# The last stage's normalisations, done in the last units of the layers for 13 of 16 batches

## The reference

```
h  = layernorm(x)                                   # 16 batches
for 4 layers:                                       # 16 heads of 64
    q = norm(h) Wq / 8 ; k = ctx Wk ; v = ctx Wv
    bias = relu(dist * Wth + bth) . Wto + bto + mask    # 32 terms per layer
    h = h + softmax(q k' + bias) v Wo
    h = h + relu(norm(h) Wf1 + bf1) Wf2 + bf2
x1 = x + tanh(g_xattn) * norm(h)                    # gated sum
f  = layernorm(x1)
out = x1 + tanh(g_ffn) * (attention(f, 16 heads of 8) + top-2 of 8 experts(f))
```

## Time and profile before

| | us |
|---|---|
| median of 3 runs (lowest, highest) | 1273.55 (1273.51, 1273.87) |
| profiled execution | 1273.89 |
| its span | 1272.1 |
| busy: PE | 1155.1 (91%) |
| busy: DVE | 1103.9 (87%) |
| busy: ACT | 1070.1 (84%) |
| busy: POOL | 804.0 (63%) |

### The profile page before, as it was taken

The page is one execution under the profiler, slowest core; times in us unless marked ns, Lnnn a source line. Parts: engine busy times, 40 slices in busy tenths (PEclk is TensorE's granted clock), DMA queues, the critical chain, the costliest instruction groups (busy, mean ns, idle before and its releaser), DMA issues.

```text
span 1272.1 us, 35758 instructions
## 1 busy us (share of the span) xinstructions
PE 1155.1 (91%) x11216; PEld 989.3 (78%) x11216; DVE 1103.9 (87%) x4455; ACT 1070.1 (84%) x3387; POOL 804.0 (63%) x917
## 2 busy tenths in 40 slices
PE   1499999999999999999999999999999999899897
PEld 1478888888888888888888888888888888666665
DVE  4988888888988888889898989898989887599996
ACT  4698888888888888888898888888888876588886
POOL 5577777777777777777777777777777733211110
PEclk9799999999999999999999999999999999899999
DMA  7400000001100000011000000000000000000000
GB/s 221 117 2 2 2 2 2 2 2 53 32 2 2 2 2 2 2 51 35 2 2 2 2 2 2 2 2 2 2 2 2 2 2 2 1 7 9 9 9 10
DMA packets 21147, 19.29 MB, mean 15 GB/s; under 512 B 5848, under 2 KB 17504, under 8 KB 20960
## 3 DMA queue, kind: packets, MB, share of 16 engines
q1 hardware_dynamic: 20960, 17.00, 4.5%
HBM read 15.95 MB, written 1.05 MB: 13 GB/s over the span
## 4 chain that ended last, share of the span: by engine, by line
PE 57%; DVE 25%; issue 8%; POOL 4%; ACT 3%; SPq 1%; DMA 1%; DVEq 0%; POOLq 0%; ACTq 0%
PE B L427 13%; PE B L392 10%; PE B L420 9%; PE B L469 9%; DVE B L844 6%; DVE sde L891 5%; DVE hh L900 4%; POOL sd L1317 3%; PE B L567 3%; PE B L406 2%; PE B L504 2%; ACT prob L753 2%; PE B L579 2%; PE B L646 2%; DVE st L881 2%
## 5 line engine op out<-in xcount | busy, mean ns | idle before, releaser
L1321 POOL TENSOR_TENSOR prob<-prob,rinv 128x512 f32<-128x512 f32 x256 | 266.6, 1041 | 266.8 <-DVE rinv L869 264.4
L692 ACT ACTIVATE prob<-score,nmax 128x128 f32<-128x128 f32 x1024 | 395.4, 390 | 9.6 <-DVE nmax L861 7.5
L682 ACT ACTIVATE relu_z<-dist_all,cst_all 128x512 f32<-128x512 f32 x356 | 276.6, 811 | 12.1 <-DMA dist_all<-in_fside_BxSxS 10.5
L861 DVE CUSTOM_DVE_ANT_0 score<-B,bias 128x128 f32<-128x128 f32 x1024 | 225.0, 284 | 42.8 <-PE B L392 42.7
L844 DVE SCALAR_TENSOR_TENSOR B<-relu_z,cst_all,B 128x512 f32<-128x512 f32 x340 | 254.4, 748 | 6.8 <-ACT relu_z L682 2.6
L692 ACT ACTIVATION_READ_ACCUMULATOR prob<-score,nmax 128x1 f32 x1024 | 194.4, 190 | 0.0
L709 ACT ACTIVATE qT<-B 128x512 f32<-128x512 f32 x128 | 76.7, 599 | 128.1 <-PE B L427 128.1
L1352 POOL TENSOR_TENSOR pool_acc<-pool_acc,clamped 128x512 f32<-128x512 f32 x140 | 178.3, 1273 | 6.7
L427 PE MATMUL B<-ctxT_all,wk 128*128 128x128 f32 x1024 | 143.5, 284 | 14.8 <-DVE nmax L861 14.1
L427 PEld LDWEIGHTS B<-ctxT_all,wk 128*128 128x128 f32 x1024 | 129.4, 197 | 25.8 <-DVE nmax L861 14.3
L406 PEld LDWEIGHTS B<-ident,prob 128*128 128x128 f32 x1024 | 120.2, 141 | 35.6 <-issue 33.4
(11 more groups left out here) (135 smaller groups left out, 2110.4 us busy)
## 6 DMA issues: line engine op xcount, KB each, us to landing
wk<-in_L_xattn_Wk SPq DMA_DIRECT2D x4, 512.0 KB, 4.5
wv<-in_L_xattn_Wv SPq DMA_DIRECT2D x4, 512.0 KB, 5.6
wq<-in_L_xattn_Wq SPq DMA_DIRECT2D x4, 512.0 KB, 5.6
wo<-in_L_xattn_Wo SPq DMA_DIRECT2D x4, 512.0 KB, 6.2
wf<-in_L_xattn_Wf SPq DMA_DIRECT2D x8, 256.0 KB, 5.0
out<-outF SPq DMA_DIRECT2D x16, 64.0 KB, 1.5
dist_all<-in_fside_BxSxS SPq DMA_DIRECT2D x1, 768.0 KB, 9.4
mask_all<-in_mask_Bx1x1xS_ff SPq DMA_DIRECT2D x1, 768.0 KB, 10.9
```

Of the source, the lines that this page charges most:

```text
L682: nc.scalar.activation(relu_z[:, j % Z_SLOTS, :], bias_flat(dist_all, g), ACT.Relu, bias=cst_all[:, l, C_BTH + k:C_BTH + k + 1], scale=cst ...
L692: last = nc.scalar.activation(prob[:, c, m, :], score[:, c, m, :], ACT.Exp, bias=nmax[:, c, m:m + 1], scale=-1.0, accum_out=rsum[:, c, m:m ...
L861: last = vec.tensor_tensor_reduce(out=score[:, c, m, :], in0=S_BANK[c][:, m * P:(m + 1) * P], in1=bias[:, u // GROUP % 2, u % GROUP, :], s ...
L1321: gp.tensor_tensor(prob[:, c, :, :], prob[:, c, :, :], rinv[:, c, :].rearrange("p (m o) -> p m o", o=1).broadcast_to([P, 4, P]), ALU.mult) ...
```

## The change

`f_first` of batch b is done in unit 51 + b, for batches 0 to 12 (units 51 to 63). Its parts come behind the unit's terms in the same four slots, not in place of them. On POOL the first root follows the layers' own root, the second follows the third slot of bias operations. The three batches left (13, 14, 15) are done in tile steps -1, 0 and 1. `x1` is written over `x_raw` and `hF` over `x_all`, batch by batch, so that neither needs to wait for an old value to be read. The tanh and the masks move from unit 60 to unit 48.

```diff
-F_EARLY = (UNITS - 3, UNITS - 2)
+F_FIRST_LAG = UNITS - BATCHES + 3
 F_FIRST_PARTS = ((0, 1), (2, 3, 4, 5, 6), (7, 8, 9), (10, 11))
...
+        x1, hF = x_raw, x_all
...
-        x1 = sb("x1", [P, GROUP, P])
-        hF = sb("hF", [P, 2, P])
...
-                    nc.tensor.transpose(M2[:, 0:P], hF[:, (i + 1) % 2, :], ident[:, :]).then_inc(fhT_done, 1)
+                    nc.tensor.transpose(M2[:, 0:P], hF[:, i + 1, :], ident[:, :]).then_inc(fhT_done, 1)
...
-                if i == UNITS - GROUP:
+                if i == UNITS - BATCHES:
                     act.wait_ge(f_gate_in, 32)
                     nc.scalar.activation(tg[:, :], gates_in[:, :], ACT.Tanh).then_inc(tanh_done, 1)
...
-                    if i in F_EARLY:
-                        for part in F_FIRST_PARTS[q]:
-                            f_first(0, F_EARLY.index(i), part)
-                    elif cur:
+                    if cur:
                         terms(plan[q])
+                        if i >= F_FIRST_LAG:
+                            for part in F_FIRST_PARTS[q]:
+                                f_first(0, i - F_FIRST_LAG, part)
...
-                    wait(dve, fout, after(g, i - GROUP, 1))
-                    vec.tensor_tensor(x1[:, i % GROUP, :], delta[:, s, :], x_raw[:, i, :], ALU.add).then_inc(fx1, 1)
+                    vec.tensor_tensor(x1[:, i, :], delta[:, s, :], x_raw[:, i, :], ALU.add).then_inc(fx1, 1)
...
-                    wait(dve, fhT_done, after(g, i - 2, 1))
-                    vec.tensor_scalar(hF[:, s, :], x1[:, i % GROUP, :], mvF[:, 1, s, 0:1], t[:, 6:7], ALU.subtract,
+                    vec.tensor_scalar(hF[:, i, :], x1[:, i, :], mvF[:, 1, s, 0:1], t[:, 6:7], ALU.subtract,
...
-                far, nxt, cur, prev = i >= 0 and f_there(g, i + 2), f_there(g, i + 1), f_there(g, i), f_there(g, i - 1)
+                far = i + 1 + UNITS - F_FIRST_LAG
+                nxt, cur, prev = f_there(g, i + 1), f_there(g, i), f_there(g, i - 1)
 
                 def first(part):
-                    if far:
-                        f_first(g, i + 2, part)
+                    if far < BATCHES:
+                        f_first(g, far, part)
...
-                if i == UNITS - GROUP:
+                if i == UNITS - BATCHES:
                     dve.wait_ge(tanh_done, 1)
...
-                if i in F_EARLY:
-                    f_root(0, F_EARLY.index(i), 0)
+                if F_FIRST_LAG <= i < UNITS:
+                    f_root(0, i - F_FIRST_LAG, 0)
...
                     norm(i, 3)
                     ops(plan[2])
-                if i in F_EARLY:
-                    f_root(0, F_EARLY.index(i), 1)
+                if F_FIRST_LAG <= i < UNITS:
+                    f_root(0, i - F_FIRST_LAG, 1)
...
-                if i >= 0 and f_there(g, i + 2):
-                    f_root(g, i + 2, 0)
-                    f_root(g, i + 2, 1)
+                far = i + 1 + UNITS - F_FIRST_LAG
+                if far < BATCHES:
+                    f_root(g, far, 0)
+                    f_root(g, far, 1)
```

More of the change, by code:

```diff
@@ L1046, in f_first @@
                     wait(dve, fh, after(g, i - 2, 1))
-                    vec.bn_stats(stF[:, 1, s, :], x1[:, i % GROUP, :]).then_inc(fbn[1], 1)
+                    vec.bn_stats(stF[:, 1, s, :], x1[:, i, :]).then_inc(fbn[1], 1)
                 elif part == 8:
@@ L1166, in f_output @@
                     wait(dve, out_st[s], (g * 2 + i // 2) * 16)
-                    vec.scalar_tensor_tensor(out=outF[:, s, :], in0=bothF[:, :], scalar=tg[:, 1:2], in1=x1[:, i % GROUP, :],
+                    vec.scalar_tensor_tensor(out=outF[:, s, :], in0=bothF[:, :], scalar=tg[:, 1:2], in1=x1[:, i, :],
                                              op0=ALU.mult, op1=ALU.add).then_inc(fout, 1)
             def f_step(g, i):
-                far, nxt, cur, prev = i >= 0 and f_there(g, i + 2), f_there(g, i + 1), f_there(g, i), f_there(g, i - 1)
+                far = i + 1 + UNITS - F_FIRST_LAG
+                nxt, cur, prev = f_there(g, i + 1), f_there(g, i), f_there(g, i - 1)
                 def first(part):
-                    if far:
-                        f_first(g, i + 2, part)
+                    if far < BATCHES:
+                        f_first(g, far, part)
                 def gates(part):
```

## The result

The changed kernel takes 1309.7 us (median of 4 runs, 1306.49 to 1311.27) against 1273.53 for the kernel before on the same chip: 1.0283 of it, interval [1.0259, 1.0307], 36 us slower. The forecast was 1310. The profiled execution is the fastest of the four: 1306.49, with a span of 1304.6.

A forecast was written before the change was run, and what follows sets the result against it. The prediction took the second half of a unit as a VectorE path and the last stage as TensorE and ScalarE; 31.8 + 0.8 + 0.8 + 1.3 + 1.9 = 36.6 us on 1273.55 gave 1310, range 1302 to 1319, eight in ten 1293 to 1325.

The forecast's parts named there:

- T: Theory of the experiments: part of the loss is the wait for POOL's second root, the rest VectorE's own work.
- The total: Whole kernel: all terms sum to 36.6 us slower, 1273.55 to 1310; chance 0.68.
- The units with terms: Units 51 to 59, which carry bias terms: added VectorE parts and the wait for POOL's second root cost 31.8 us.
- The forecast's own range: Whole kernel: 1302 to 1319 us, from bounds of the wait for POOL and of the blocked operations.
- Units 60 and 63, and the seam: Unit 60 +0.8, unit 63 +0.8, and tile step -1, doing all of batch 13, +1.3 us.
- the two terms that were put at 2.1: Unit 63 at +0.8 us and the seam (tile step -1) at +1.3 us.
- The tanh: End of unit 48: VectorE waits for a tanh behind ScalarE's three relus, +1.9 us; unit 60 gives back 0.1 at most.
- The last stage: Tile steps 2 to 13 lose `f_first` work on VectorE but stay at 10.16 us: gain 12 x 0.
- The upper bound of 11.2: Tile steps 2 to 13: most they could gain if all VectorE time removed counted, 12 x 0.93 us.
- Rival C: Stretched units: TensorE's clock falls there, granted clock under 1.00 between 884 and 1090 us; chance 0.10.
- the range for eight in ten: Whole kernel: 1293 to 1325 us, from rival A (1295, no deciding POOL wait, chance 0.12) to just short of Rival C.

The follow-up runs named there:

- swap: Changed kernel with POOL issuing the second root ahead of the third slot of bias operations, not behind it: 1301.86 us, ratio 1.0204.
- both: swap plus, in unit 48, ScalarE's tanh issued ahead of the last three relus instead of behind them: 1300.03 us, ratio 1.0184.
- late: Changed kernel with the layout of spread for twelve batches in units 50 to 63, both roots moved, tanh as in both: 1297.24 us, ratio 1.0171.
- lag60: Changed kernel with early normalisations begun in unit 60 instead of 51: batches 0 to 3 there, twelve in tile steps: 1280.76 us, ratio 1.0036.
- tanh48: Kernel before with only the tanh and the masks moved from unit 60 to unit 48: 1275.45 us, ratio 1.0008.
- spread: Kernel before with its two early normalisations laid out over three units and both roots placed where POOL is free: 1273.66 us, ratio 0.9993.
- after_again: The changed kernel, unedited, run again on another chip for a second profile: 1311.26 us, ratio 1.0273.

## Why the prediction was right, step by step

One sum over units 51 to 59 shows it, for each kernel against the kernel before (nine rows of the same cut each; VectorE busy 130.54 before):

| | length | more than before | VectorE busy more | the rest |
|---|---|---|---|---|
| before | 146.03 | | | |
| after | 176.98 | 30.95 | 20.42 | 10.5: 13.1 of waits for the root, 2.6 of other idle time gone |
| swap | 168.47 | 22.44 | 22.88 | -0.4 |
| both | 167.36 | 21.33 | 22.63 | -1.3 |
| late | 171.16 | 25.13 | 28.24 | -3.1 |

So T holds: two thirds of the units' loss is VectorE's own work, one third the place of one root in POOL's list. With the wait gone the units lengthen by what VectorE does more, within 3 us over nine units. The last column is a net: old idle time that has gone, less new short gaps between the parts and, in `swap`, a longer wait for scores; that it is as small as -0.4 there is chance.

**The total** (36.6 forecast, 36.2 by the medians). The mechanism is right, but the agreement to 0.4 is partly luck. In the two profiled executions the terms come to 33.5, 3 under the forecast: 30.95 in units 51 to 59, 0.47 in unit 60, 0.43 from unit 63 on, 1.85 in unit 48, less 0.24 in unit 49. (The spans differ by 32.5, since the kernel after reaches unit 48 1.0 earlier, on a part of the program that the change does not touch.) The median is 3.2 above the profiled execution of the kernel after, and the other profiled execution of this program has 4.6 more ahead of tile step 1, at a clock of 0.74 against 0.95, for which the forecast had no term. The two errors cancel.

**The units with terms** (31.8 forecast, 30.95 measured). By unit, forecast and measured: 51 4.2 and 4.20; 52 3.8 and 3.03; 53 3.8 and 3.86; 54 3.0 and 3.23; 55 4.2 and 4.18; 56 3.8 and 3.04; 57 3.8 and 3.86; 58 3.0 and 3.18; 59 2.2 and 2.37. Units 52 and 56 were over-sized by 0.8: their five operations hold one long addition, not two as those of unit 53, and the forecast had taken unit 53's list for all four. That is 0.47 of it (from the fourth reciprocal to the next score 6.88, 917.48 to 924.36, for 7.35). The other 0.3 lies ahead of that reciprocal, where the unit grew by 1.03 and not by 1.35; what is held there changed, as follows.

**A cancellation that was not forecast.** The first root stands on POOL between the layers' root and the next normalisation of probabilities, and it has changed who is held beside whom on VectorE. All instances in units 51 to 59 after (ns, shortest/median/longest):

```profile
L892 DVE TENSOR_SCALAR sde<-sd x9: 169/169/171, 891.9 to 1051.0; 128x2 f32<-128x2 f32 x9
L901 DVE TENSOR_SCALAR hh<-x_all,mv,rs x18: 333/1154/1306, 892.3 to 1052.5; 128x128 f32<-128x128 f32 x18
L1035 DVE TENSOR_TENSOR tinyF<-tinyF,tg x9: 159/396/885, 894.7 to 1053.9; 128x1 f32<-128x1 f32 x9
L1039 DVE TENSOR_SCALAR delta<-x_all,mvF,tinyF x9: 346/444/461, 895.2 to 1054.1; 128x128 f32<-128x128 f32 x9
```

The inverse deviation, mostly 1.00 before, is 0.17 everywhere. In unit 51 it ran from 891.11 to 892.11 before, to 0.02 behind the end of POOL's normalisation of probabilities (891.05 to 892.09); in the kernel after it starts at 891.93, beside the small root (891.87 to 892.42). The first of the two normalisations behind it is held instead (both in units 54 and 58), in unit 51 for 1.17 from 892.34 on, to 0.09 behind the end of POOL's (892.38 to 893.42); the median of all 18 is 1.15, and was 0.57 in the kernel before. So is the product with the gate (0.16 in unit 61 before): its longest, 0.89, ends at 915.63, 0.02 behind an addition of POOL. These come to about nothing.

The forecast's own range, 1302 to 1319, also had a bound for blocked operations. No run shows that term: `delta` took 0.46 at most in the kernel after, 0.12 over its shortest 0.35, beside POOL's residual bias sum. That `delta` can be held shows in `late` (0.73), and `hF` in `swap` (1.21). Where each instruction fell beside POOL's list decided here how long it took, and the place of one root changed that for the inverse deviation and the normalisations.

**Units 60 and 63, and the seam** (0.8 + 0.8 + 1.3 forecast). Unit 60: 0.47 (15.71), against 0.78 in `lag60`; TensorE has 15.17 left to do in it here and 15.49 there. From the start of unit 63 to the end of the span: 195.45 against 195.02, 0.43 for the two terms that were put at 2.1. That step was mis-sized, or it can't be sized from single executions: the stretch to tile step 1 is 34.82 in the kernel before and 34.88 and 34.91 in `tanh48` and `spread`, all at a granted clock of 0.85, which comes to about 10 us of half rate; it is 35.33 in the kernel after (0.95, so 4), 36.59 in `swap` and `lag60` (0.91, about 6), and 39.92 in after_again (0.74, about 20). The lengths of half rate are estimates from the granted clock of these stretches. What the parts of step -1 cost at an equal clock stays open.

**The tanh** (1.9): 1.85 in the kernel after, 1.83 alone in `tanh48`, and 1.8 back in `both`. The mechanism is as the earlier trace rows had it: VectorE waits for a tanh that stands behind ScalarE's relus (2.13 in `tanh48`). The forecast left out what unit 49 gives back, 0.24.

**The last stage** (12 x 0): the steps take 10.16 with 1.46 less on VectorE. The forecast had read 0.93 from steps 13 and 14, and 8.55 for a step without the parts; but step 14 of the kernel before still finishes work left over from step 13 (an addition to `accF` at 1244.16, for one). The upper bound of 11.2 should have been 17.5. At a worth of zero the sum does not change. What it waits for there, in the steps 11 and 12 of the kernel after:

```profile
PE B L568 <- ACT prob L754: 2.0, 2, 1.0
...
DVE nmaxF L1066 <- PE B L568: 2.0, 2, 1.0
```

TensorE's scores wait for ScalarE's exponentials, once a step; VectorE's maxima wait for the scores. Most of the work taken from VectorE has become that idle time (0.5 in steps 13 and 14 of the kernel before, 2.0 here).

**Rival C** came in part and cost at most 0.1 in a unit of the changed kernel. The clock fell to 0.91 in units 53 and 54 of the kernel after, and to 0.91 or 0.92 in 51, 52, 57 and 58 of after_again. Unit 53 takes 19.99 at 0.91 and, in after_again, 19.96 at 1.00: VectorE was waiting for POOL anyway (1.89 and 1.88). Only when that wait was taken away (`swap`) did the half rate show, with 0.55 in unit 52 of `swap`. The upper end of the range for eight in ten, 1325, was put just short of what C would cost, and no run shows that cost: the runs showed this 0.1 and this 0.55.

## What to carry to other kernels

Work that is moved off a stage is worth what that stage's path gets, not the busy time that falls: ask which engine's piece stands in the chain there, and here it was TensorE and ScalarE. Where it goes, count the receiving engine's whole busy time as soon as that engine is the path for half of a unit, and look for a unit where it isn't: the same twelve parts cost 2.5 us in a unit with terms even when nothing waited for their roots, 0.8 in one without, and nothing there once they stood behind the last thing that anyone waits for. A helper's instruction was here as late as all that was queued ahead of it in its engine's fixed list (the second root of unit 53 at 943.32, behind five bias operations from 938.35 on), and that can be summed from the list before the change is made.

## What the runs showed of the hardware

Two executions differed in TensorE's clock at the same place. Unit 52 of `swap` and `both`, the same code, fell to a granted clock of 0.50 (from 916.5 to 919.5) in one and kept 1.00 in the other, behind an idle of 1.95 and 1.96 us. The seam of the changed kernel took 35.33 us at 0.95 in one execution and 39.92 at 0.74 in another, by the estimate above 4 and about 20 us of half rate. That moved the whole kernel by 4.6 us, so a change whose effect is of that size should be judged by its own stretch. And a wait in the shadow of a longer one hid the lower clock: unit 53 took 19.99 at 0.91 and 19.96 at 1.00, with VectorE waiting 1.89 and 1.88 for POOL in it.
